# Plain fp32 products, column sums on DVE and one degree product in a one-core graph layer

## What is computed

```python
xn = layernorm(x)
# graph part: a sum per destination node, divided by the root of the node's degree
m   = xn[src] @ Wg[:256] + edge_attr @ Wg[256:]
deg = segment_sum(1, dst);  norm = where(deg > 0, rsqrt(max(deg, 1)), 0)
gnn = segment_sum(m * norm[dst][:, None], dst) + h_bias
# mixing part: linear attention, 8 heads of 32
q, k, v = split(xn @ w_qkv + b_qkv);  k = ln(k) * kln_g + kln_b;  v = ln(v) * vln_g + vln_b
kv  = einsum('bhnd,bhne->bhde', k, v) / 6250
mix = gelu((q @ kv + xn) @ w1 + b1) @ w2 + b2 + xn
x   = x + gnn + mix
x   = x + ffn(layernorm(x))     # feed-forward over the two experts that a router chooses
```

## Time and profile before

| | us |
|---|---|
| median of 3 runs | 1610.23 |
| lowest, highest | 1606.24, 1611.78 |
| span of the profiled execution | 1630.3 |

### The profile page before, as it was taken

One profiled execution on the slowest core, in us unless ns is written; L12 is line 12 of the kernel. 1 busy time (PEld: TensorE's weight loads), 2 busy tenths in 40 slices (PEclk: granted clock), 3 DMA queues, 4 the chain that ended last, 5 costly groups with the idle time before them and its releaser, 6 DMA issues.

```text
span 1630.3 us, 22836 instructions
## 1 busy us (share of the span) xinstructions
PE 1173.3 (72%) x7416; PEld 803.1 (49%) x7416; DVE 654.6 (40%) x1698; ACT 559.7 (34%) x1157; POOL 915.7 (56%) x975
## 2 busy tenths in 40 slices
PE   0157767776686777766676767677776839999997
PEld 0033333433343343334445444453554539999997
DVE  5633223323223333221233244243432446676775
ACT  4731111111111111111333343333342457677674
POOL 6166666666666666666666666666666103344342
PEclk9988987888788888778798897889898959999999
DMA  9976666656665666486677787777777341222221
GB/s 234 319 216 202 181 194 185 205 177 180 201 193 174 189 199 181 127 260 204 206 225 232 220 240 248 225 223 241 234 225 238 103 136 40 71 61 76 64 68 39
DMA packets 209235, 295.03 MB, mean 181 GB/s; under 512 B 20940, under 2 KB 180146, under 8 KB 207887
## 3 DMA queue, kind: packets, MB, share of 16 engines
q1 hardware_dynamic: 152899, 165.66, 34.7%
q0 software_dynamic: 39888, 108.97, 22.1%
q10 hardware_dynamic: 16350, 19.20, 3.5%
HBM read 261.75 MB, written 32.00 MB: 180 GB/s over the span
## 4 chain that ended last, share of the span: by engine, by line
another core or an unknown queue 31%; PE 30%; issue 14%; DVE 9%; ACT 9%; DVEq 2%; DMA 2%; SPq 2%; ACTq 1%; POOL 0%; POOLq 0%
PE bank L1156 8%; PE bank L1167 8%; PE bank L944 2%; PE bank L997 2%; PE bank L938 2%; DVEq L1324 2%; PE bank L930 2%; PE bank L1003 1%; ACT fl L649 1%; PE bank L1041 1%; ACT L751 1%; ACT L731 1%; DVE acc L1326 1%; DVE xc L1339 1%
## 5 line engine op out<-in xcount | busy, mean ns | idle before, releaser
L583 POOL DMA_INDIRECT ring<-xn_table,src_sb x807 | 781.8, 969 | 465.7 <-issue 221.1
L930 PE MATMUL bank<-ring,s 128*32 128x512 f32 x1662 | 283.6, 667 | 65.3 <-DVE s L1298 42.6
L944 PE MATMUL bank<-fl_t,wg 128*128 128x128 f32 x1120 | 158.7, 300 | 51.6 <-ACT fl_t L649 36.7
L944 PEld LDWEIGHTS bank<-fl_t,wg 128*128 128x128 f32 x1120 | 146.7, 211 | 54.8 <-ACT fl_t L649 38.8
L938 PE MATMUL bank<-ident,fl 128*128 128x128 f32 x280 | 60.9, 356 | 146.9 <-ACT fl L649 131.7
L1326 DVE TENSOR_TENSOR acc<-acc,bank 128x96 f32 x277 | 70.7, 255 | 226.5 <-issue 87.4
L938 PEld LDWEIGHTS bank<-ident,fl 128*128 128x128 f32 x280 | 39.3, 177 | 222.2 <-ACT fl L649 170.7
L1331 DVE TENSOR_TENSOR xt_lo<-bank,xt_hi 128x250 fp32r<-128x250 f32 (+1 forms) x75 | 37.9, 505 | 260.7 <-ACT xt_hi L649 173.0
L649 ACT ACTIVATE xt_hi<-bank 128x250 fp32r<-128x250 f32 (+1 forms) x75 | 33.4, 446 | 285.6 <-remote 227.3
L712 ACT ACTIVATE kvn<-xc 125x512 f32<-125x512 f32 x50 | 31.5, 630 | 262.1 <-DVE xc L1339 135.3
L1156 PE MATMUL bank<-xf_hi,fw_hi 128*128 128x256 f32 x400 | 113.5, 284 | 9.4 <-DVE fw_lo L1628 7.2
(11 more groups left out here) (221 smaller groups left out, 2374.1 us busy)
## 6 DMA issues: line engine op xcount, KB each, us to landing
ring<-edges SPq DMA_DIRECT2D x207, 512.0 KB
ring<-xn_table,src_sb POOLq DMA_INDIRECT x807
xnr<-xn_table SPq DMA_DIRECT2D x50, 125.0 KB
xnr<-xn_table SPq DMA_DIRECT2D x25, 250.0 KB
xch<-x SPq DMA_DIRECT2D x25, 250.0 KB
base_rows<-xch ACTq DMA_DIRECT2D x25, 250.0 KB
x_rows<-xch ACTq DMA_DIRECT2D x25, 250.0 KB
xt_cols<-xte ACTq DMA_DIRECT2D x25, 250.0 KB
```

Of the source, the lines that this page charges most:

```text
L583: pool.indirect_dma_start(out=to, out_offset=None, in_=rows, in_offset=bass.IndirectOffsetOnAxis(ap=index, axis=0),).then_inc(done, 16)
L930: mm = pe.matmul(ps_seg[t % 2][j * W:(j + 1) * W, :], lhsT=s32[:, t % 3, j * TS + i, :].bitcast(F32), rhs=ring[:, u, j, :], start=i == 0, ...
L944: mm = pe.matmul(ps_y[:, o * P:(o + 1) * P], lhsT=wg[:, c, o * P:(o + 1) * P], rhs=fl_t[:, c, :], start=c == 0, stop=c == 3)
```

## The change

- Key/value and mixing products take the fp32 operands as they are. `wkv_hi`, `wkv_lo`, `m_hi`, `m_lo`, `w2_hi`, `w2_lo`, `xt_lo`, `hm_hi` and `hm_lo` are gone, with the ACT copies and DVE subtractions that made them, and so is the wait for them. `keys` issues 2 fp32 matmuls in place of 6 of fp32r; `mix_first` and `mix_second` issue 4 each in place of 12, of 250 columns where the first operand was padded to 256.
- ACT's copy of the turned rows goes to `xt`, which has two buffers; it waits for the product before the last.
- The column sums of `kvn` are added up on DVE in `ksum`, an instruction of 125x512 behind each `normed`; one product with ones at the last tile sums the partitions. `accumulate` waits for the addition (s_ks).
- The three rows of the one-hot matrix are added on DVE (`strip_counts`, two instructions of 128 elements a partition for each group), and one fp32r product a group makes the degrees in place of three. strip_counts(t+1) stands at the third step of group t, ahead of the key/value pieces, and waits for project(t-1); project(t) waits for it. `one_hot` waits for the strip sums of two groups before in place of the projection.

```diff
             def strip_counts(t):
+                m = len(strips(t))
+                v.wait_ge(s_hot, t + 1)
+                wait_past(v, s_pj, t - 1)
+                hot = s32[:, t % 3, 0:m * TS, :].rearrange("p (j i) w -> p j i w", i=TS)
+                v.tensor_tensor(pair[:, 0:m, :], hot[:, :, 0, :], hot[:, :, 1, :], ALU.add).then_inc(s_pr, 1)
+                v.wait_ge(s_pr, t + 1)
+                v.tensor_tensor(counts[:, t % 2, 0:m * W]..., pair[:, 0:m, :], hot[:, :, 2, :], ALU.add).then_inc(s_cnt, 1)
             def normed(n):
+                v.wait_ge(s_kvn, n + 1)
+                v.wait_ge(s_ks, n + 1)
+                v.tensor_tensor(ksum[:, :], ksum[:, :], kvn[:, n % 2, :], ALU.add).then_inc(s_ks, 1)
             def project(t):
-                for i in range(TS):
-                    pe.matmul(ps_y[:, KC * P:KC * P + n], lhsT=ones_r[:, :], rhs=hot[:, 0:len(strips(t)), i, :], start=i == 0, stop=i == TS - 1)
+                pe.wait_ge(s_cnt, t + 1)
+                pe.matmul(ps_y[:, KC * P:KC * P + n], lhsT=ones_r[:, :], rhs=counts[:, t % 2, 0:n], start=True, stop=True)
             def keys(n):
-                pe.wait_ge(s_xlo, n + 1)
+                pe.wait_ge(s_xev, n + 1)
-                ops = [(a[:, c, 0:TN], b[:, c, :]) for c in range(KC) for a, b in products((xt_hi, wkv_hi), (xt_lo, wkv_lo))]
+                for c in range(KC):
+                    mm = pe.matmul(ps_kv[0:TN, :], lhsT=xt[:, n % 2, c, 0:TN], rhs=wstage[:, c, :], start=c == 0, stop=c == KC - 1)
             def accumulate(n):
-                pe.wait_ge(s_kvn, n + 1)
-                pe.matmul(ps_f[0:1, :], lhsT=ones[0:TN, 0:1], rhs=kvn[:, n % 2, :], start=n == 0, stop=n == NT - 1, skip_group_check=True)
+                pe.wait_ge(s_ks, n + 2)
+                if n == NT - 1:
+                    pe.matmul(ps_f[0:1, :], lhsT=ones[0:TN, 0:1], rhs=ksum[:, :], start=True, stop=True)
             def turned(n, width):
-                    wait_past(act, s_kvp, n)
+                    wait_past(act, s_kvp, n - 1)
-                copy(xt_hi[:, :, 0:width], ...).then_inc(s_xhi, 1)
+                copy(xt[:, n % 2, :, 0:width], ...).then_inc(s_xev, 1)
             for q in range(TS * STEPS):        # DVE
                 if i == 0 and t + 1 < NG:
                     one_hot(t + 1)
+                if i == 2 and t + 1 < NG:
+                    strip_counts(t + 1)
...
-                if kv_at(q, 0) is not None:
-                    turned_lo(kv_at(q, 0), TN)
-                if mix_at(q, 2) is not None:
-                    mixed_lo(mix_at(q, 2))
-                if mix_at(q, 0) is not None:
-                    turned_lo(NT + mix_at(q, 0), CN)
```

More of the change, by code:

```diff
@@ L116, in gps_layer @@
         ring = sbe("ring", [P, RS, ST, 2 * D])
-        s32 = sbe("s32", [P, 3, GT, W], F32R)
+        s32 = sbe("s32", [P, 3, GT, W])
+        pair = sbe("pair", [P, ST, W])
+        counts = sbe("counts", [P, 2, P], F32R)
         ones_r = sbe("ones_r", [P, P], F32R)
@@ L146, in gps_layer @@
         xte = sbe("xte", [P, 2, KC, CN])
-        xt_hi = sbe("xt_hi", [P, KC, CW], F32R)
-        xt_lo = sbe("xt_lo", [P, KC, CW], F32R)
+        xt = sbe("xt", [P, 2, KC, CN])
         st6 = sbe("st6", [TN, BLK, 6])
@@ L168, in gps_layer @@
         sbk = alloc(kv_part)
-        wkv_hi = sbk("wkv_hi", [P, KC, 2 * D], F32R)
-        wkv_lo = sbk("wkv_lo", [P, KC, 2 * D], F32R)
+        ksum = sbk("ksum", [TN, 2 * D])
         wstage = sbk("wstage", [P, KC, 2 * D])
@@ L181, in gps_layer @@
         sbm = alloc(mix_part)
[L182 to L185 removed]
         w2_sb = sbm("w2_sb", [P, KC, D])
[L187 to L189 removed]
+        hm = sbm("hm", [P, KC, CN])
         mix_part.close()
@@ L574, in _ @@
             pool.wait_ge(s_mask, 1 + P // HC)
-            for t in (xt_hi, xt_lo):
-                pool.memset(t[:, :, :].bitcast(F32), 0.0).then_inc(s_const, 1)
+            pool.memset(xt[:, :, :, :], 0.0).then_inc(s_const, 1)
             edges_of = [0] + [min(ST * d, NS) for d in DONE[:-1]] + [NS]
@@ L910, in _ @@
             pe.transpose(ps_t[0:1, 0:P], okc[:, 2:3], ident[:, :]).then_inc(s_dp, 1)
-            pe.matmul(ps_acc[:, 0:KC * P], lhsT=xt_hi[:, 0, 0:P], rhs=xt_lo[:, 0, :], start=True, stop=True, skip_group_check=True)
+            pe.matmul(ps_acc[:, 0:KC * P], lhsT=xt[:, 0, 0, 0:P], rhs=xt[:, 1, :, 0:P], start=True, stop=True, skip_group_check=True)
             def products(hi, lo):
@@ L1396, in fold @@
                     v.tensor_tensor(kv_t[:, :, :], kv_t[:, :, :], block_mask[:, :].unsqueeze(1).broadcast_to([P, KC, P]), ALU.mult).then_inc(s_c, 1)
-                    for pad in (hm_hi, hm_lo):
-                        v.memset(pad[:, :, CN:CW].bitcast(F32), 0.0)
                 if step == 2:
```

101 lines of the change are left out of this document (36 added, 65 removed).

## The result

| | before | after |
|---|---|---|
| median | 1610.25 us (5 runs) | 1606.49 us (5 runs) |
| lowest, highest | 1606.24, 1611.99 | 1604.58, 1609.96 |
| span of the profiled execution | 1630.3 | 1604.4 |

The ratio is 0.9966, 95% interval 0.9950 to 0.9981: faster. The medians are 3.8 us apart, the ratio makes it 5.5, and I had forecast 23.

A forecast was written before the change was run, and what follows sets the result against it. PE's order of work and late matmul completions together were taken to set the pace, gathers 15% below. Terms -18 + 9 - 7 - 9 - 2 + 4 = -23 us gave 1607 profiled, 1587 us plain; 8-in-10 range 1546 to 1630.

The forecast's parts named there:

- PE's work as work: PE's busy work was to fall by 36 us in the key/value stage and rise by 18 us in mixing.
- Half of it is time (-18, +9): Half of PE's work change counted as time: -18 us in the key/value stage, +9 us in mixing.
- PE as the pacer: Rival: PE alone sets the pace and its 36 us come back whole; 1548 us, chance 0.13.
- The chain of turned_lo (-7): Key/value stage: the step between ACT's copy and the product goes, 14 waits times 0.5; -7 us (0 to -35).
- the start (-2): Start: the strips' second one-hot on DVE no longer waits behind wkv_lo, 88.9 to 86.8; -2 us (0 to -2).
- The chain of hm_lo (-9): Mixing: hm_hi and hm_lo go from between gelu and the second product; -9 us (0 to -12).
- mixing's work (+9): Mixing stage: PE's work rises by 18 us (28 - 10), half of it counted as time; +9 us.
- DVE's new work (0): DVE: 75 us added and 55 removed on an engine busy a third of these stages; no time counted.
- the gathers (+4): POOL's gathers stretched by DVE operations with two SBUF inputs: 8.7 us, half on the path; +4 us (0 to 9).
- The strip counts' wait: DVE: strip_counts(t+1) waits for project(t-1); counted 0, or 25 us if the covering step is gone.
- slower: the gathers: Rival: each two-SBUF-input DVE operation stops the gather beside it as long as it runs, 37 us; 1620 us, chance 0.07.
- nothing moves: Rival: late completions end when POOL stops, so a quicker PE waits longer; 1610 us, within 5, chance 0.12.

The follow-up runs named there:

- b_again: The kernel before, unchanged, run and profiled a second time; 1613.1 us, 1.0007 of before.
- p_again: p_fp32 unchanged, run again on a chip where before takes 1628.1 us; 1614.8 us, 0.9928 of before.
- p_keys: The kernel before with only the key/value products in plain fp32, mixing left in halves; 1625.7 us, 0.9984 of before (1628.1 us).
- p_fp32: The changed kernel without DVE's additions: column sums and three degree products a group stay on PE; 1605.1 us, 0.9949 of before (1612.6 us).
- x_gath0: p_fp32 with all gathers behind the first six units, except the last group's, replaced by plain DMAs on SP's queue; 1362.0 us, 0.9244 of before (1475.2 us).
- x_keyshalf: The changed kernel with the second of each tile's two key/value products left out; 1482.7 us, 1.0055 of before (1475.2 us).
- x_keys2: p_fp32 with each tile's two key/value products issued twice; 1471.7 us, 0.9972 of before (1475.2 us).
- x_chain: p_fp32 with the two steps between gelu and the second mixing product put back as plain copies; 1472.0 us, 0.9963 of before (1475.2 us).
- u_degree: The changed kernel with three degree products a group back on PE, no pair sums on DVE; 1604.6 us, 0.9955 of before (1612.6 us).
- a_third: The changed kernel unchanged, run again on a chip where before takes 1475.6 us; 1482.8 us, 1.0052 of before.
- a_again: The changed kernel unchanged, run again on a chip where before takes 1628.1 us; 1620.5 us, 0.9959 of before.
- p_third: p_fp32 unchanged, run a third time, where before takes 1475.2 us; 1472.7 us, 0.9982 of before.
- run 21: Not a run's label: in "over the whole run 21 of its gathers", 21 counts gathers of x_keys2 that start beside a running L1323.

## Why the prediction was wrong

*PE's work as work: right.* 34 us less in the key/value stage against b_again, 40 against the earlier trace rows; I had 36. The column sums are 54 for 57, the key/value products 22 for 31, the degree product 7.5 for 10. For the mixing products p_again and p_keys compare on one chip, 720 to 1250 us: 393.42 against 380.17 us. That is +13 for my +28, but the clock rose with it, from 0.84 to 0.89; times clock it is 350 against 319 us, +31 where I had 24 at the full clock, and p_again got 8 gathers further in that stretch (358, 350). So this term was not too large.

*Half of it is time (-18, +9): this is the step that failed.* The share is 0. I had two rivals in one number, PE as the pacer and stops that end with POOL, and split the difference. But the split had no row behind it: I had the stops of PE and of POOL side by side and no price for either. What I passed over is in the earlier trace rows. PE is busy 432 us at a granted clock of 0.84, and 432.34 x 0.84 = 363 us is roughly what that work would take at the full clock; the gathers' floor, in my own text, is 499. An engine with 363 us of work beside one with 499 is not the pacer, and a part of its busy time is only its low clock. The estimate is fair: p_fp32's 449.11 x 0.85 = 382 us became 363 us of stage (103.2 to 466.3) in x_gath0, with the gathers gone. And the ladder of x_keyshalf to x_keys2 shows the clock rising with the work. I had divided every price by 0.84, as though the clock were given.

*The chain of turned_lo (-7) and the start (-2).* p_keys has both and is at 0.9984, so they bring 2.6 us (0.5 to 5) together. PE's 69.3 us of waiting for xt_lo (50.8 in b_again) were in the main the late completion, named after the engine that came last. After the change that time and more stands with fl and xt.

*The chain of hm_lo (-9) with mixing's work (+9).* I had the sum at 0, and it was -9 us on one late chip (by the ratios of p_again and p_keys) and -8 on the other (594.1 against 586.3 us). The chain is sized right if the +9 is struck out with the other half; but x_chain could not show it on a prompt chip, so it is consistent and no more. A rival stands beside it. hm_lo was itself an operation on two SBUF tiles, and the gathers that started while it ran lost 5.7 us in b_again and 4.8 in p_keys. The mean gather from 720 to 1250 us falls from 973 ns (b_again, p_keys) to 962 (p_fp32) and 967 (p_again), which over some 360 gathers is 2 to 4 of the 8 to 9 us. What else is the chain through hm_hi and hm_lo, and what the missing xt_lo, no run separates.

*DVE's new work (0) and the gathers (+4).* The strip counts' wait did no harm: u_degree, without it, is at 0.9955, within the others. The additions' cost is 5 us where completions are late and 10 where they are not. Stretched gathers are the right mechanism for 6 of it. I had taken 8.7 and halved it with the same factor as PE's work; on a prompt chip POOL is the pacer, so there it counts whole. The rival "slower: the gathers" was priced at 1620 by a gather blocked for as long as the addition runs; the one shown overlaps the addition for 0.45 us and is stretched by 0.32, and the one before it overlaps another and isn't stretched at all. The Trainium skill's page "SBUF — State Buffer", section "SBUF: two separate sides", says that whichever of the two starts first gets the port pair for the whole instruction and the other is blocked. The traces here bear it out in one direction: a gather that starts second is longer (1091 ns against 945 in a_third), and by less than the whole operation of 692; DVE, when it starts second, is not (692 ns). And the whole, 5 to 9 us of 807 gathers, is far below the 37 us that I had made of it. The rival's sign won all the same: where POOL's cadence alone is the pace, the change is slower.

*The rival "nothing moves".* It had 1610 within 5 us and a chance of 0.12; 1606.5 came. Its reason, completions that end when POOL stops, is supported by the waits that did not shrink (124 or 145 us before, 150 after), by the seventh slot without use, and by five kernels of one stage length. It is not shown: the run that would have shown it, no gathers on a late chip, did not fall on one.

With the measured terms for a late chip, 0 for PE's work, -3 for key/value chain and start, -9 for mixing and +5 for the additions, the sum is -7 us; by their ratios a_again has -6.7 and the first result -5.5 (-3.8 by the medians). The terms are taken from a_again's own chip, so only the first result is a check of them. That the change came out faster, as forecast, is no merit of the forecast: its largest term is nothing, and the gain lies in its smaller ones. On a prompt chip the products bring -2.7 (p_third) and the additions cost 10, and a_third has +7.7.

A kernel that beats both is p_fp32: the change without the column sums and the pair sums on DVE. It is at 0.9949, 0.9928 and 0.9982 of before, and after is at 0.9966, 0.9959 and 1.0052.

## What to carry to other kernels

Before counting an engine's saved work as time, multiply its busy time by its granted clock and set that beside the floor of the other engines; here 363 us stood beside 499, and 122 us of busy time between the least and the most PE work (184 at the full clock) did not push the end of the stage back. Work moved off a loaded engine onto an idle one is not free when the idle one shares something with the pacer: DVE was idle most of the stage, and its additions of two SBUF tiles made those gathers longer that started while they ran. An addition that starts just behind a gather's start cost it nothing here; a kernel that places them so was not tried. And when two causes for a stall are open, give them as two cases; a factor of one half between them is a number that no mechanism gives.

## What I had not expected of the hardware

- The same kernel takes 1475 us on three chips and 1613 to 1628 on two, and only on those two, and in the first result, are completions of matmuls seen late, up to 11 us. The change is 0.4% faster on the one kind and 0.5% slower on the other, so one chip's ratio does not carry over.
- TensorE's clock followed its work: 0.81 of full speed on average at 351 busy us in 500, 0.86 at 380, 0.93 at 412, 0.99 at 473, and 1.00 where it was busy 369 of 370. Between the levels of 1.2 and 2.4 GHz 0.81 means 62% of the stretch at the upper one. The gathers beside it came no later with more work on PE; x_keys2's were even shorter than p_third's (957 against 966 ns in that stretch, from 378.78/396 and 379.82/393); over the whole run 21 of its gathers start beside a running L1323, the last step of kvn, and lose 3.4 us, where in p_third 31 lose 6.9.
- A plain fp32 product of 512 columns is two instructions: four of them, two products, took 1.88 us at full clock, where six fp32r products take 1.38 by the earlier trace rows. It needs no halves, and where PE has room that is the better trade.
